# Second layer: six elementwise steps from GpSimd to VectorE, the score's clamp behind its exponential, sums of squares without pairs

## The reference, cut to what matters

```
h     = layernorm(x) * (1 + c) + s
z     = conv4(h @ W_in)                       # 4 taps along the tokens, causal
val, gate, s_raw = z[0:128], silu(z[128:256]), z[256:]
p     = exp(clip(scale * s_raw, -20, 20))
p_w   = p * time_w
poly  = w0 + w1*val - w2*val^2
num   = cumsum(p_w * poly * cos(val*theta)), the same with sin    # 4 thetas: 8 planes
den   = cumsum(p_w)
re,im = num / max(den, 1e-4)
y     = rms_norm(re, im over a head) @ W_re, W_im
x     = x + ga * ((y * gate) @ W_out)
h     = layernorm(x) * (1 + c') + s'
f     = relu(h @ W_fc)^2 @ W_proj
x     = x + gb * (spikes of 5 leaky steps driven by f) / 5
```

## Time and profile before

| | us |
|---|---|
| median of 3 runs (all: 2256.86, 2245.25, 2257.46) | 2256.86 |
| the profiled execution's own time | 2251.27 |
| its span, first to last instruction | 2249.5 |
| busy in the span: PE / DVE / ACT / POOL | 1976.5 / 1624.6 / 866.7 / 925.0 |
| start of the second layer's instructions in the span | about 1882 |
| mean granted TensorE clock | 0.928 of full |

### The profile page before, as it was taken

How to read it: one execution, slowest core, us unless ns; L and a number is a source line. 1 busy time by engine, 2 the same in 40 slices (tenths; PEclk the granted TensorE clock), 3 DMA queues, 4 the chain that set the end, 5 groups by cost and what they waited for, 6 DMA issues and landing times. The chain is left out here.

```text
span 2249.5 us, 43858 instructions
## 1 busy us (share of the span) xinstructions
PE 1976.5 (88%) x16447; PEld 1324.3 (59%) x16455; DVE 1624.6 (72%) x3595; ACT 866.7 (39%) x1694; POOL 925.0 (41%) x917
## 2 busy tenths in 40 slices
PE   4898997998898898898899799989899997778886
PEld 2573563564565465466456357667899996334443
DVE  6969769749948948957966983532367766999995
ACT  2031332233234134234123222223356654777784
POOL 2523413632541551541451353130566664554452
PEclk7998999999999899989989989999999999889998
DMA  3000000000000000000000000312422223010000
GB/s 113 11 1 15 2 2 16 9 14 15 4 20 15 1 21 17 1 21 7 10 17 6 16 8 15 105 35 107 168 72 72 70 74 93 19 38 24 5 12 17
DMA packets 70179, 72.47 MB, mean 32 GB/s; under 512 B 12977, under 2 KB 58593, under 8 KB 69841
## 3 DMA queue, kind: packets, MB, share of 16 engines
q1 hardware_dynamic: 61296, 51.75, 7.7%
q0 software_dynamic: 8672, 17.91, 2.3%
HBM read 38.05 MB, written 27.43 MB: 29 GB/s over the span
## 5 line engine op out<-in xcount | busy, mean ns | idle before, releaser
L669 ACT ACTIVATE a_prep<-ps 128x1536 f32<-128x1536 f32 (+1 forms) x112 | 155.6, 1390 | 332.2 <-PE ps L1304 217.1
L897 DVE TENSOR_REDUCE a_mpart<-ps 128x4 f32<-128x512 f32 (+1 forms) x320 | 190.8, 655 | 46.8 <-PE ps L1245 33.5
L1839 ACT ACTIVATE b_hid<-ps,b_stage 128x128 f32<-128x128 f32 x572 | 163.6, 368 | 139.2 <-PE ps L1954 139.2
L476 POOL TENSOR_TENSOR a_K<-a_K,a_yU 128x480 f32<-128x480 f32 (+14 forms) x120 | 83.5, 696 | 315.3 <-DVE a_yU L842 314.2
L1824 POOL DMA_INDIRECT rows_y<-b_orow,b_target x143 | 164.0, 1147 | 119.4 <-DVE b_orow L1929 116.6
L482 POOL TENSOR_TENSOR a_X<-a_X,a_txy 128x480 f32<-128x480 f32 (+14 forms) x240 | 181.5, 772 | 61.4 <-DVE a_txy L847 59.9
L1117 PE MATMUL ps<-a_txy,cst 128*128 128x480 f32 (+14 forms) x480 | 175.7, 471 | 13.4 <-DVE a_txy L829 12.7
L1954 PE MATMUL ps<-b_hTp,b_stage 128*128 128x128 f32 x1144 | 152.8, 277 | 0.0
L1963 PE MATMUL ps<-b_stage,b_hid 128*128 128x128 f32 x1144 | 151.7, 276 | 0.3 <-ACT b_hid L1839 0.3
L864 DVE TENSOR_TENSOR a_mats<-ps,cst 128x512 f32<-128x512 f32 x112 | 69.9, 684 | 109.8 <-PE ps L1146 109.8
L1559 POOL DMA_INDIRECT rows_h<-a_mats,r_slot x112 | 111.1, 992 | 74.8 <-DVE a_mpart L897 51.2
(11 more groups left out here) (466 smaller groups left out, 4609.8 us busy)
## 6 DMA issues: line engine op xcount, KB each, us to landing
b_hrow<-rows_h SPq DMA_DIRECT2D x143, 65.0 KB, 1.8
b_w<-in_wexp SPq DMA_DIRECT2D x16, 514.0 KB, 9.9
d_got<-rows_y SPq DMA_DIRECT2D x32, 256.0 KB, 3.8
rows_h<-a_txy SPq DMA_DIRECT2D x19, 325.0 KB, 3.1
rows_y<-b_orow,b_target POOLq DMA_INDIRECT x143, 2.4
out<-xs SPq DMA_DIRECT2D x8, 256.0 KB, 2.3
cst<-in_const SPq DMA_DIRECT2D x1, 1865.5 KB, 15.2
rows_h<-a_mats,r_slot POOLq DMA_INDIRECT x112
```

The source lines that it names most:

```text
L669: nc.scalar.activation(Pt[:, at:at + width, :], ps[:, 4:4 + width, :], ACT.Exp).then_inc(e_exp.sem, width)
L897: nc.vector.tensor_reduce(mpart[:, i, j, 4 * g:4 * g + 4], ps[:, 4 + n % 4, :].rearrange("p (r j) -> p r j", r=4)[:, :, 0:128 if i != j el ...
L1839: last = nc.scalar.activation(hid[:, p % 2, f, :], ps[:, p % 2, 128 * f:128 * f + 128], ACT.Gelu, bias=stage[:, p % 3, AT_B1 + f:AT_B1 + f ...
```

## The change

- `gather`: VectorE does all four steps for every sample; GpSimd has none.
- A new stream `weights` (letter p) on VectorE: the clamp, pw, curve and denm, four steps per sample.
- The score: ScalarE takes the exponential straight out of the bank, with scale and bias; VectorE then clamps the exponential between exp(-20) and exp(20). The copy and the separate exponential become one instruction; the buffer sraw goes.
- The pairs go: TensorE multiplies each of the eight squares by the head matrix, eight products per sample in place of four (and the one of den as before). A square waits for the product that used its buffer four squares earlier, not for the pair.
- GpSimd keeps `scaled`, now first in its stream, and `spikes`.
- All four strings are new. VectorE's now begins with six g (all of sample 0's gather and the two additions of sample 1), and its step k (four copies of gates out of banks, L2350) comes after g, f, d instead of first.

```diff
+SCORE_LOW, SCORE_HIGH = math.exp(-20.0), math.exp(20.0)
 ORDER_C, VectorE, the beginning:
-    've': ('kggggfffgkkdgkfgkfffgffffmmmmmmmmmmmmmmmfmmmfffffffmmgmmbmmmmmbmbmbbmfbff...
+    've': ('ggggggffgfggdkkgkkpkfpfpmffffffggpmpmmmmmmmpmmmmfmmmfffpmffmfgfbpgmmmmmmg...
-    'po': ('ggggfffmgkgmffgmmfkmmfmmffmmmmggffgmfmgmsmmfmfmfgsmsmfgmsfmgfmmmmsffsfmmmmmmsfsffmmssmmmmmssssss'),
+    'po': ('kkssssssssssssssss'),
 ScalarE
-                nc.scalar.activation(sraw[:, :], ps[:, ZS, :], ACT.Identity, bias=col[:, 0:1],
-                                     scale=wts["sscale"]).then_inc(e_sraw.sem, 1)
+                nc.scalar.activation(prob[:, :], ps[:, ZS, :], ACT.Exp, bias=col[:, 0:1],
+                                     scale=wts["sscale"]).then_inc(e_p.sem, 1)
...
-                act.wait_ge(*e_clip(b))
-                if b:
-                    act.wait_ge(*e_pw(b - 1))
-                nc.scalar.activation(prob[:, :], sclip[:, :], ACT.Exp).then_inc(e_p.sem, 1)
...
-                        act.wait_ge(*e_pair(b, (n - M) // 2))
+                        act.wait_ge(*e_sum(b, n - M))
 VectorE, gather: for every b
+                ve.wait_ge(*e_got[b % 2](b // 2))
+                nc.vector.tensor_tensor(rows[:, 0:2, :, :], rows[:, 0:2, :, :], rows[:, 2:4, :, :], ALU.add)...
+                yield
+                ve.wait_ge(*e_comb(b, 0))
+                nc.vector.tensor_tensor(rows[:, 0, :, :], rows[:, 0, :, :], rows[:, 1, :, :], ALU.add)...
 VectorE, new
+            def weights(b):
+                ve.wait_ge(*e_p(b))
...
+                nc.vector.tensor_scalar(sclip[:, :], prob[:, :], SCORE_HIGH, SCORE_LOW, ALU.min, ALU.max)...
+                yield
...
+                nc.vector.tensor_tensor(pw[:, :], sclip[:, :], timew[:, :], ALU.mult).then_inc(e_pw.sem, 1)
+                yield
...
+                nc.vector.tensor_tensor(curve[:, :], slope[:, :], val[:, :], ALU.mult).then_inc(e_curve.sem, 1)
+                yield
...
+                nc.vector.tensor_scalar(denm[:, :], den[:, :], 1e-4, None, ALU.max).then_inc(e_denm.sem, 1)
 TensorE, middle, after each of the eight mixing products
-                    if n % 2 == 0:
-                        continue
-                    yield
-                    pe.wait_ge(*e_pair(b, n // 2))
+                    yield
+                    pe.wait_ge(*e_nsq(b, n))
                     if b:
                         pe.wait_ge(*e_lr(b - 1))
-                    mm(ps[:, SUM, :], con("block4"), npair[:, n // 2 % 2, :], start=n == 1, stop=False)...
+                    mm(ps[:, SUM, :], con("block4"), nsq[:, n % M, :], start=n == 0, stop=False)...
```

More of the change, by code:

```diff
@@ L198 @@
 ORDER_C = {
[L199 to L205, removed]
@@ L214, in each @@
-def each(stream, samples=range(B)):
-    for b in samples:
+    'pe': ('wwwwwwwwwwwwwwwwwwwwwwwwwwwwwwwwwwwwwwwwwwwwfffffffmmfmmmmmmmmmmmmmfmmffmbfmmmbmmmbmbbmbmmmmmbbmmfmb'
+           'bmffmbmfmmbmmbmbmbmmmbmmmmbbbmfmbfbfmmbfbmbmmmmbmmbmmmmmmmbbbfbmfbfmmmmmbfbbmmmbmbmmmmbmfbmbmbmfbfmb'
+           'mfmmbmbmbmmbmmmmmbmbbmfmbfbfmmbfbbmmmbmmmbmmmmmmbbmmmbbmmmmbmmmmmbmmbbmbmbmmmbbbbmbbbbbbbbbb'),
+    've': ('ggggggffgfggdkkgkkpkfpfpmffffffggmpmmmmmmmpmmmmfmmmfffpmffmfgfbpgmmmmmmgmpbmbmbbmmbgmfmfmmffpmfmffpm'
+           'pmmfpmmbmmmmmgmssmgmbmbmmpbbsbsfmgmpmfpfffsgffmmpfmmmbmmmgmbgmbgbbgbmmmfgpssmmpmmmfgffpfffsfgmsmbmmp'
+           'smmgsmbmmbmmbbmpsbfpmffspfmmmsfmmfmpfmfsmmbmmmgmmbmgbbbbmmmfmmffgpmspmffgffmsmppfmmmsssmmmmbbbmbbbps'
+           'mmmfpmsfsmmmpfsfmmmmmpmmmbmsmmmmbmmbbbsbmsfmssmmmbsbbbbsbsssssssss'),
@@ L217, in each @@
+    'act': ('ffffffffffffffffffffmmmffmfffmmfffmfmfffmffffmfmbbfmmfffbfbmmffmbffmbfbfbmbbffmffbbfbmmfbmmmbmbfffff'
+            'fbbfmfmbmffbbmbmfbbfffbbfbfmfmbbbmmmbmbfffffbmffbmbfbfbffbmfffmbffbbmfmmbbmbmbffbfffffbmmffbbbffbmbm'
+            'bmfffbfbfmfbmbbmmbmbmffffbfffffbbfbfmffbbmfbfbmfmbmfmbbmbmmbbffffbmffbfmfmbfbfffmfbbbfbmbmmmbbmmbmmb'
+            'bbmbbbbmbbbmbbbbbbbbbbbbbbbb'),
+    'po': ('kkssssssssssssssss'),
+}
+def each(stream, n=B):
+    for b in range(n):
         yield from stream(b)
@@ L2089, in layer1 @@
         e_prod, e_num, e_nsq = ev("prod", 2 * M), ev("num", 2 * M), ev("nsq", 2 * M)
-        e_pair = ev("pair", M)
-        e_den, e_denm, e_dsq, e_mix, e_sum = ev("den"), ev("denm"), ev("dsq"), ev("mix", 2 * M), ev("sum", M + 1)
+        e_den, e_denm, e_dsq, e_mix, e_sum = ev("den"), ev("denm"), ev("dsq"), ev("mix", 2 * M), ev("sum", 2 * M + 1)
         e_lr, e_rs, e_yg, e_yT, e_o, e_x = ev("lr"), ev("rs"), ev("yg"), ev("yT"), ev("o"), ev("x")
@@ L2119, in scaled @@
                 nc.gpsimd.tensor_scalar(gate3[:, :, :], gate3[:, :, :], 1.0 / STEPS, None, ALU.mult).then_inc(s_gates.sem, 1)
-            def front(b):
-                po.wait_ge(*e_sraw(b))
-                if b:
-                    po.wait_ge(*e_p(b - 1))
-                nc.gpsimd.tensor_scalar(sclip[:, :], sraw[:, :], 20.0, -20.0, ALU.min, ALU.max).then_inc(e_clip.sem, 1)
-                yield
[L2127 to L2154, removed]
             def spikes(b):
@@ L2167, in spikes @@
                 nc.gpsimd.tensor_tensor(xb, xb, tokens(ya[:, :]), ALU.add).then_inc(e_end.sem, 1)
[L2169 to L2178, removed]
+            weave(ORDER_C["po"], k=scaled(), s=each(spikes))
         @block.scalar
@@ L2401, in front @@
                                                ALU.mult).then_inc(e_gate.sem, 1)
+            def weights(b):
+                ve.wait_ge(*e_p(b))
+                if b:
+                    ve.wait_ge(*e_pw(b - 1))
+                nc.vector.tensor_scalar(sclip[:, :], prob[:, :], SCORE_HIGH, SCORE_LOW, ALU.min, ALU.max).then_inc(e_clip.sem, 1)
+                yield
+                ve.wait_ge(*e_clip(b))
+                if b == 0:
+                    ve.wait_ge(*s_time())
+                if b:
+                    ve.wait_ge(*e_den(b - 1))
+                    ve.wait_ge(*e_poly(b - 1))
+                nc.vector.tensor_tensor(pw[:, :], sclip[:, :], timew[:, :], ALU.mult).then_inc(e_pw.sem, 1)
+                yield
+                ve.wait_ge(*e_lin(b))
+                ve.wait_ge(*e_val(b))
+                if b:
+                    ve.wait_ge(*e_poly(b - 1))
+                nc.vector.tensor_tensor(curve[:, :], slope[:, :], val[:, :], ALU.mult).then_inc(e_curve.sem, 1)
+                yield
+                ve.wait_ge(*e_den(b))
+                if b:
+                    ve.wait_ge(*e_dsq(b - 1))
+                nc.vector.tensor_scalar(denm[:, :], den[:, :], 1e-4, None, ALU.max).then_inc(e_denm.sem, 1)
             def middle(b):
@@ L2476, in spikes @@
                                                    ALU.add).then_inc(e_spk.sem, 1)
-            weave(ORDER_C["ve"], g=each(gather), d=derived(), k=gates(), f=each(front), m=each(middle), b=each(back), s=each(spikes))
+            weave(ORDER_C["ve"], g=each(gather), d=derived(), k=gates(), f=each(front), p=each(weights), m=each(middle), b=each(back), s=each(spikes))
         @block.tensor
```

36 lines of the change are left out of this document (12 added, 24 removed).

## The result

| | before | after |
|---|---|---|
| median, us | 2255.32 (2245.25 to 2257.46) | 2218.86 (2215.66 to 2220.52) |
| ratio to before | | 0.9845, 95% interval 0.9813 to 0.9878 |
| profiled execution: time, span | 2251.27, 2249.5 | 2215.66, 2213.9 |
| busy PE / DVE / ACT / POOL | 1976.5 / 1624.6 / 866.7 / 925.0 | 1987.5 / 1591.5 / 860.9 / 787.3 |

The change is worth 36 us, and 35.6 between the two profiled executions. Of these, 4.8 us lie in the first layer, whose code is the same (its end came at 1877.0 in place of 1881.8); the same changed kernel, run once more (a1_again), has it at 1881.6, so it is scatter. The second layer went from 367.7 to 336.9 us: 30.8 us.

A forecast was written before the change was run, and what follows sets the result against it. VectorE's queue, stretched by GpSimd's SBUF accesses, was taken to set the pace in the second layer's middle. Relief and added work -26.2, TensorE and score +4, start +3.4, end +2.6 gave -16 us: 2236, forecast 2226 to 2245, range 2217 to 2256.

The forecast's parts named there:

- rival B: Second layer: relief arrives whole and TensorE's additions lie in gaps; 2222 us, chance 0.18.
- signs of being wrong in kind: Changed kernel: VectorE's instructions stay as long as they are, or VectorE is idle more than TensorE.
- Step 1: VectorE, second layer: GpSimd-caused stretching goes, 52.2 us in six groups, 57 with small ones; 8.5 stays.
- rival D: VectorE: the stretching isn't GpSimd's doing, or what stays of GpSimd suffices; about 2278 us, chance 0.05.
- Step 2: VectorE takes on planes, pw, curve, clamp and denm: 31.0 us more work; its balance with the relief -26 us.
- Step 3: TensorE gets four more products per sample, 27.5 us; 4 us on the path, bounds 0 and 24.
- Step 4: Score path: shorter chain gains nothing; VectorE may stand at sample 1's clamp, 1 us allowed within TensorE's 4.
- Step 5: Layer start: gate copies placed later +2.5 us, waiting for sample 1's planes +0.9, `scaled` nothing; sum +3.4 us.
- Step 6: Sample 7's last scans: about three of TensorE's four more sums stand on the path, +2.6 us.
- parts 3 to 6: Added costs: TensorE's products and score path 4 us together, start 3.4, end 2.6.
- Rival E: VectorE's queue: relief turns into waits at clamps, planes or squares; 2247 us, chance 0.22.
- Rival C: Samples 1 to 6: TensorE becomes the bound, sums finding no gaps before the next convolutions; 2265 us, chance 0.10.

The follow-up runs named there:

- a1_again: The changed kernel run once more, unaltered, on another chip: 2216.3 us, ratio 0.9851 to the kernel before.
- e3_half: Changed kernel without TensorE's products of sums for the even planes, 32 fewer (half the squares left out of the norm): ratio 0.9860 to the kernel before.
- e9_fused: Changed kernel with spikes also on VectorE, the lower clamp on ScalarE, upper clamp and pw in one VectorE instruction: 2218.3 us, ratio 0.9841 to the kernel before.
- e1_load: Changed kernel plus 78 two-input GpSimd additions on private tiles that nobody waits for: 2272.4 us, ratio 1.0093 to the kernel before.
- e10_silent: Kernel before with GpSimd's clamp, curve, pw, denm, pairs and planes of samples 1 to 7 on 8 columns instead of 512: ratio 0.9760 to the kernel before.
- e5_gatesfirst: Changed kernel with VectorE's four copies of the gates moved back to the front of its string: ratio 0.9859 to the kernel before.
- e4_oldorder: Changed kernel's instructions with all four strings in the old kernel's interleaving: ratio 0.9985 to the kernel before.
- e8_peold: Changed kernel with only TensorE's string in the old interleaving: ratio 0.9972 to the kernel before.
- e2_pairs: Changed kernel with GpSimd adding the squares in pairs again and TensorE doing four products of sums per sample, not eight: ratio 0.9991 to the kernel before.

## Why the prediction was right, and where its sum was off

The direction, the main mechanism (GpSimd's silence relieves VectorE) and the range were right. The forecast itself was not: 2218.9 lies below its 2226 to 2245 and near the lower end of the range, which reached there for rival B. Rival B, 2222 with a chance of 0.18, says what came: the relief whole, TensorE's additions in gaps. (Its sum takes off 6 us besides, which no row gives.) The gain was forecast at 16 us for the layer and was 31, and most steps that were off erred the same way.

One of the prediction's own signs of being wrong in kind came true: after the change VectorE is idle more than TensorE in the middle, 24.4 us for 11.7. VectorE's queue set the pace before, and its relief is the gain; that it still sets it afterwards, as the forecast's picture has it, isn't shown. Relieving TensorE (e3_half) brings nothing, and neither does relieving VectorE a little further (e9_fused).

**Step 1, stretching that goes: right.** The six groups of the earlier trace rows had 60.7 us of (mean minus median) times count; the same six now have 64 x 0.060 + 64 x 0.044 + 32 x 0.024 + 8 x 0.118 = 8.4 us by the rows above (the counts and the layernorm have none), where 8.5 was forecast. GpSimd as the cause is shown by e1_load and e10_silent, so rival D is out. The Trainium skill's rule (GPSIMD Engine Reference, Specifications) of contention with VectorE instructions of two SBUF inputs agrees: in e1_load, with the load back, L2412's successor L2448, which reads a bank, takes 658/672/691 ns, though three of the eight start inside a two-input GpSimd operation. The earlier trace rows also have L2389 stretched (485 ns for 342), which reads one tensor; whether it falls under the rule's other half, a two-port mode, no row shows. The page gives no price; the runs do, 0.50 and 0.61 us of VectorE per us of a two-input operation.

**Step 2, work that VectorE gets, and the balance of both: mis-sized by 7 us.** The durations were right (0.418, 0.682, 0.679, 0.420). But VectorE's busy time fell by 33.3 us (321.1 to 287.8), not by 26. The term adds durations, and the records of consecutive plain instructions overlap, as in this timeline of the changed kernel (start us, us):

```profile
1918.86 0.67 DVE L2397 TENSOR_TENSOR c_prod<-c_poly,c_sn 128x512 f32<-128x512 f32 x1
1919.56 1.22 DVE L2403 TENSOR_TENSOR_SCAN c_num<-c_ones,c_prod 128x512 f32<-128x512 f32 x1
1920.70 0.67 DVE L2397 TENSOR_TENSOR c_prod<-c_poly,c_sn 128x512 f32<-128x512 f32 x1
```

The second product starts 0.08 us before the scan in front of it ends. Summed over the layer's records, the overlap grew from 29.4 to 33.9 us: 4.5 of the 7. The durations themselves fell by 28.7 us (350.4 to 321.7), 2.5 more than forecast. e10_silent shows the same side: there they fell by 64 us with the overlap unchanged (29.2), where the rows had given 57: 56 in the six groups (52 forecast) and 8 in the smaller ones (5 allowed).

**Step 3, TensorE: 4 us forecast, none shown (e3_half).** VectorE's idle time in the middle rose by 2.5 us in one execution and fell by 0.7 in a1_again. I had reckoned in full-clock units, 88% full, and read that as crowded. What I missed is that the granted clock of the middle would rise, from 0.92 to 0.99. 0.92 means that 16% of 302 us, 48 us, ran at the lower of the two levels (1.2 GHz); after, some 5 us. TensorE's busy time times the clock rose by 27 us (227 to 255), the size of the added products, its busy time by only 10. The added products aren't the whole cause of the rise: without them it is 0.96 (e3_half), and with TensorE's old work beside a quicker VectorE 0.98 (e10_silent). The Trainium skill's other rule, the weight-load share as the better metric (Trainium Kernel Development and Optimization, Performance Expectations), would have given the right term, 0; but the share is 48% in a stretch that is 96% busy, so that it hit by reading room isn't shown.

**Step 4, the wait at sample 1's clamp: right in place.** It is 2.8 us in the profiled execution and 1.2 in a1_again; 1 us was allowed.

**Step 5, the start: 3.4 forecast, 2.5 measured, with a wrong account.** The waits for planes came (2.3 and 1.1 us), but e5_gatesfirst shows that moving the copies back gives nothing. What I priced at nothing is `scaled`: its two operations stretch pw of sample 0 by 2.2 us and the next angle by 0.8, in VectorE's queue ahead of the first product. That this is what the start pays is read from the timeline; no run moves them.

**Step 6, the end: 2.6 forecast, 1.7 and 0 measured.** From the start of the last scan to the output product it is 10.6 us before, 12.3 in the changed kernel and 10.6 in a1_again, and VectorE waits 0.9, 3.7 and 2.1 us there for the last mixing product. The execution with 12.3 had TensorE at a clock of 0.81 to 0.85 between 2160 and 2170, a1_again at 1.00. The stretch from the output product on is 27.9 for 28.2 us.

The account of the 14.6 us by which the layer was mis-forecast: VectorE's busy time fell by 33.3 us, not 26.2, and its idle time rose by 2.5 us, not by the 10.0 of parts 3 to 6. That is 7.1 and 7.5.

**Rival E was nearer than it looked.** Its 0.22 was for a relief that turns into waits. e4_oldorder and e8_peold are that rival: the same instructions, the same relief, and 0 or 13 us of the 31. So more than half of the gain hangs on the new strings. I had priced only their beginning; that they would let the relief through was an assumption, and TensorE's string at least must fit the others (e8_peold). **Rival C** (TensorE the bound) did not come: TensorE's idle time in the middle went from 54.8 to 11.7 us, far below the 29 at which C begins.

## What to carry to other kernels

If one shape of a VectorE instruction has a median at its minimum and a mean a third above, lay GpSimd's operations beside the long ones before counting GpSimd as spare capacity: a two-input GpSimd operation cost VectorE 0.7 us on average in e1_load (1.47 us long) and 1.0 in e2_pairs (1.6 us long), as much as doing the work itself (0.68) or more, and can be waited for on top. What paid here was the work that left both engines, the pairs (e2_pairs). When the queue that sets the pace gets lighter, re-derive the order of the others too: with one old string more than half of the gain was gone. And when TensorE gets work, look at its granted clock before and after as well as at its busy time.

## What was not expected of the hardware

- A one-input GpSimd operation took longer (1.92 us against 1.47 for two inputs of the same size, beside the same VectorE program) and stretched VectorE less, 0.18 against 0.50 us per us.
- A VectorE instruction of two SBUF inputs that starts inside a two-input GpSimd operation doesn't share the way but stands until it ends: in the kernel before 17 of 20 products, and in e1_load 15 of 17, end 0.55 us after GpSimd's end; 13 of 18 scans and 12 of 14 end 1.08 us after it.
- TensorE got 27 us of added products and only 10 us more busy time, as the granted clock of the stretch rose from 0.92 to 0.99; the part of that rise that came without the products is 0.92 to 0.96 (e3_half).
